# First loads moved to the SyncE queue in f32, with a cast on ScalarE; bv and two combined weights later

## What is computed

```python
q = x @ Wq + bq            # 16 heads of 64
k = x @ Wk + bk            # 2 key heads of 64, 8 query heads share each
v = x @ Wv + bv
scores = q . k over a window of 256 keys, 128 to each side
out    = softmax(scores) @ v
x = layernorm(x + out @ Wo + bo)
# a complex-valued linear layer; W_real and W_imag come from small factors G1, G2
out_real = x_real @ W_real.T - x_imag @ W_imag.T + bias_real
out_imag = x_real @ W_imag.T + x_imag @ W_real.T + bias_imag
x = layernorm(x + concat(out_real, out_imag))
```

## Time and profile before

| | before |
|---|---|
| median of 3 runs | 491.24 us (491.09 to 491.98) |
| profiled execution, its own time | 491.3 us |
| span of its slowest core (core 2) | 489.8 us |
| spans of the 8 cores | 484.1 to 489.8 us |
| TensorE busy | 459.2 us, 94% |
| VectorE busy | 390.8 us, 80% |
| ScalarE busy | 316.8 us, 65% |
| GpSimd busy | 170.0 us, 35% |

### The profile page before, as it was taken

One profiled execution on the slowest core, in us unless ns is written; L12 is line 12 of the kernel. 1 busy time (PEld: TensorE's weight loads), 2 busy tenths in 40 slices (PEclk: granted clock), 3 DMA queues, 4 the chain that ended last, 5 costly groups with the idle time before them and its releaser, 6 DMA issues.

```text
span 489.8 us, 11362 instructions; the slowest of 8 cores (484.1 to 489.8 us)
## 1 busy us (share of the span) xinstructions
PE 459.2 (94%) x3832; PEld 216.9 (44%) x3832; DVE 390.8 (80%) x619; ACT 316.8 (65%) x398; POOL 170.0 (35%) x118
## 2 busy tenths in 40 slices
PE   0698999999999999999999999999999999899994
PEld 0454444444444444444444444444444444344542
DVE  0193678688887988798887988788887888899985
ACT  0136766566776767767676667666766677777653
POOL 8100044343334323443334334432333233333360
PEclk9999999999999999999999999999999999899998
DMA  6999985545664556646664556546642345556333
GB/s 59 160 168 172 217 209 109 108 118 121 150 153 99 140 131 151 144 99 147 151 151 99 134 138 150 136 102 152 151 117 78 111 128 130 153 150 130 87 87 129
DMA packets 82808, 65.15 MB, mean 133 GB/s; under 512 B 67776, under 2 KB 68288, under 8 KB 82752
## 3 DMA queue, kind: packets, MB, share of 16 engines
q1 hardware_dynamic: 75984, 51.17, 40.3%
q0 software_dynamic: 6768, 13.26, 18.4%
HBM read 44.63 MB, written 16.78 MB: 125 GB/s over the span
## 4 chain that ended last, share of the span: by engine, by line
PE 82%; DVE 6%; issue 5%; DMA 3%; ACT 3%; POOL 1%; DVEq 0%; ACTq 0%; POOLq 0%
PE pW L428 22%; PE pW L507 19%; PE pW L493 13%; PE pW L459 9%; PE pS L438 9%; DMA XT<-xt 3%; PE pW L418 3%; PE pW L413 2%; PE pW L476 2%; ACT EX L651 1%; DVE st L805 1%; DVE xb L800 1%; DVE xr L800 1%; PE pS L507 1%; PE pW L402 1%
## 5 line engine op out<-in xcount | busy, mean ns | idle before, releaser
L651 ACT ACTIVATE EX<-pS,shift 128x2048 bf16<-128x2048 f32 x96 | 188.5, 1964 | 58.4 <-PE pS L438 58.4
L376 POOL TENSOR_TENSOR xb<-x,beta_b 128x1024 f32<-128x1024 bf16 x32 | 69.2, 2161 | 159.9 <-DVE x L882 150.9
L428 PE MATMUL pW<-XT,wq_sb 128*128 128x512 bf16 x512 | 120.1, 379 | 0.4 <-DMA XT<-xt 0.2
L507 PE MATMUL pW<-wo_sb,attnT 128*128 128x512 bf16 x496 | 118.2, 384 | 0.0
L384 POOL TENSOR_TENSOR xr<-xr,bo_b 128x1024 f32<-128x1024 f32 x32 | 75.6, 2362 | 121.7 <-DVE EX L777 101.3
L638 ACT ACTIVATE QT<-pW,bq_sb 128x512 bf16<-128x512 f32 x64 | 44.0, 687 | 60.7 <-PE pW L428 59.0
L777 DVE TENSOR_TENSOR EX<-EX,mask_s 128x2048 bf16<-128x2048 bf16 x64 | 80.1, 1252 | 3.3 <-ACT EX L651 3.1
L852 DVE TENSOR_TENSOR xb<-pW,xb 128x1024 f32<-128x1024 f32 x48 | 58.8, 1225 | 17.6 <-PE pW L493 11.2
L507 PEld LDWEIGHTS pW<-wo_sb,attnT 128*128 128x128 bf16 x496 | 45.7, 98 | 60.2 <-issue 14.1
L428 PEld LDWEIGHTS pW<-XT,wq_sb 128*128 128x128 bf16 x512 | 46.0, 98 | 48.4 <-issue 1.8
L459 PEld LDWEIGHTS pW<-VB,EX 128*128 128x128 bf16 x1512 | 50.1, 97 | 27.1 <-issue 26.1
(11 more groups left out here) (77 smaller groups left out, 365.0 us busy)
## 6 DMA issues: line engine op xcount, KB each, us to landing
xr<-x SPq DMA_DIRECT2D x32, 512.0 KB, 3.9
y<-xb SPq DMA_DIRECT2D x31, 512.0 KB, 3.0
XT<-xt POOLq DMA_DIRECT2D x32, 256.0 KB, 5.2
wq_sb<-wq POOLq DMA_DIRECT2D x8, 256.0 KB, 21.8
wo_sb<-wo POOLq DMA_DIRECT2D x4, 512.0 KB, 36.8
bo_b<-bo SPq DMA_DIRECT2D x1, 512.0 KB, 10.5
beta_b<-beta SPq DMA_DIRECT2D x1, 512.0 KB, 5.7
y<-xb SPq DMA_DIRECT2D x2, 256.0 KB, 2.1
```

The source lines that it names most:

```text
L376: gp.tensor_tensor(xb[:, r1 % 4 * D:(r1 % 4 + 1) * D], x1[:, r1 % 2 * D:(r1 % 2 + 1) * D], beta_b, ALU.add).then_inc(gp_b, 1)
L428: i = pe.matmul(p, wq_sb[:, t * 1024 + c * 128:t * 1024 + (c + 1) * 128], rhs_x(g, c), start=c == 0, stop=c == 7)
L507: i = pe.matmul(ps, attnT[:, p % 2 * D + c * 128:p % 2 * D + (c + 1) * 128], wo_sb[:, half * 4096 + c * 512:half * 4096 + (c + 1) * 512], ...
L651: act.activation(EX[:, e0:e0 + 2048], pS, AF.Exp, bias=shift).then_inc(act_e, 1)
```

## The change

wk and x tiles 0 and 1 leave GpSimd's queue. SyncE loads them in f32, as its first three transfers, into `xb`; ScalarE copies each into `wk_sb` or `XT` as bf16 when it has landed, and TensorE's first half waits for the three copies (`act_h`). A tiny instruction ahead of them on ScalarE makes the table load early. dmask goes behind bq and bk; bv goes behind the wait for x tile 3, ahead of mask, and has a semaphore of its own. `wd` moves from the end of step 0 into step 1, `wsn` into step 2. As tiles 0 and 1 no longer count on `d_xt[0]` and `d_xt[1]`, later waits for these expect one round less.

```diff
         def _(sp):
-            sp.dma_start(dmask, dmask_d).then_inc(d_dmask, 16)
+            sp.dma_start(xb[:, 0:D], wk_d).then_inc(d_wk, 16)
+            for t in range(2):
+                sp.dma_start(xb[:, (t + 1) * D:(t + 2) * D],
+                             xt_d[t * 128:(t + 1) * 128, :]).then_inc(d_x0[t], 16)
             sp.dma_start(bq_sb, bq_d).then_inc(d_const, 16)
             sp.dma_start(bk_sb, bk_d).then_inc(d_const, 16)
-            sp.dma_start(bv_b, ap(bv_d, 0, [[0, 128], [1, 128]])).then_inc(d_const, 16)
+            sp.dma_start(dmask, dmask_d).then_inc(d_dmask, 16)
             sp.wait_ge(d_xt[3], 16)
+            sp.dma_start(bv_b, ap(bv_d, 0, [[0, 128], [1, 128]])).then_inc(d_bv, 16)
             sp.dma_start(mask, mask_d).then_inc(d_mask, 16)
...
-            gp.dma_start(wk_sb, wk_d).then_inc(d_wk, 16)
-            load_x(0)
-            load_x(1)
             gp.dma_start(wv_sb, wv_d).then_inc(d_wv, 16)
...
-            pe.wait_ge(d_wk, 16)
...
-                for t in range(2 * h, 2 * h + 2):
-                    pe.wait_ge(d_xt[t], 16)
+                if h == 0:
+                    pe.wait_ge(act_h, 3)
+                else:
+                    pe.wait_ge(d_xt[2], 16)
+                    pe.wait_ge(d_xt[3], 16)
...
-            act.wait_ge(d_const, 3 * 16)
+            act.wait_ge(dve_i, 1)
+            act.activation(nm1[:, 0:1], eps, AF.Copy)
+            act.wait_ge(d_wk, 16)
+            act.activation(wk_sb, xb[:, 0:D], AF.Copy).then_inc(act_h, 1)
+            for t in range(2):
+                act.wait_ge(d_x0[t], 16)
+                act.activation(XT[:, t * D:(t + 1) * D], xb[:, (t + 1) * D:(t + 2) * D], AF.Copy).then_inc(act_h, 1)
+            act.wait_ge(d_const, 2 * 16)
             k_out(0)
...
-            v.wait_ge(d_const, 3 * 16)
+            v.wait_ge(d_bv, 16)
             v_out(0, 4)
...
                     if r < 0:
+                        if s == 1:
+                            v.wait_ge(*emptied(("G", 3)))
+                            v.tensor_tensor(wd, wit, wrt, ALU.subtract).then_inc(dve_g, 1)
+                        if s == 2:
+                            v.tensor_tensor(wsn, witn, wrt, ALU.subtract).then_inc(dve_g, 1)
                         masked(s, 1)
...
                         if s == 0:
                             gate_out(2)
                             gate_out(3)
-                            v.wait_ge(*emptied(("G", 3)))
-                            v.tensor_tensor(wd, wit, wrt, ALU.subtract).then_inc(dve_g, 1)
-                            v.tensor_tensor(wsn, witn, wrt, ALU.subtract).then_inc(dve_g, 1)
```

More of the change, by code:

```diff
@@ L132, in build_nc @@
     d_wk = sem("d_wk")
+    d_bv = sem("d_bv")
+    d_x0 = [sem(f"d_x0_{i}") for i in range(2)]
+    act_h = sem("act_h")
     d_wv = sem("d_wv")
@@ L544, in _ @@
                 if j == 0 and s < Q_END:
-                    new_x = [(d_xt[t % 8], (t // 8 + 1) * 16) for t in range(4 * g + 4, 4 * g + 8)]
+                    new_x = [(d_xt[t % 8], (t // 8 + (1 if t % 8 >= 2 else 0)) * 16) for t in range(4 * g + 4, 4 * g + 8)]
                 else:
@@ L692, in _ @@
                 q_out(n)
-            act.wait_ge(dve_i, 1)
             n_ln = 0
```

## The result

The changed kernel takes 494.56 us (median of 4 runs, 494.19 to 494.82) against 491.24 us before: slower, by a ratio of 1.0067 (95% interval 1.005 to 1.0084). Times and ratios are those of the chip's usual state; single executions in its slower one (here 555.92 us, of the kernel before) are left out. The forecast was 489.5 us with a range of 487.2 to 493.8. Both the sign and the range were missed.

What follows compares the result with a forecast made beforehand. TensorE, busy 94% of the span, bounds the kernel and its head shifts the whole span. Gates at 26.3 + 462.0 - 0.9 = 487.4, plus 0.6 for the worst head: 488.0, plus 1.5 beyond the span: 489.5 us; range 487.2 to 493.8.

Steps and rivals of the forecast that it cites:

- x tile 3: 13.8 forecast: In the head, x tile 3 would land at 13.8 us, with ends of 11.5 and 19.4 us.
- the case of every core: In the head, all cores would be near core 7's undisturbed 15.38 us once bv goes behind x tile 3.
- 1.2 us of free window: From 2.0 to about 3.2 us SyncE's f32 tiles would move at 377 GB/s: 0.86 of a tile, 1.3 us gained.
- part 3: Moving wd and wsn to steps 1 and 2 would end the second av block's wait in step 1: -0.9 us.
- bv's landing: Behind x tile 3, bv would land 7.2 us after its issue, priced by mask's 7.0 us.
- bv lands as late as before: Rival: behind x tile 3 bv takes 12 us; up to 4.8 us more, 492 to 494.3 us; chance 0.12.
- the rival with a gap of 4 us: Rival: TensorE idles some 4 us ahead of the gates; a clock fall costs 1.7 us, giving 488.9; chance 0.14.
- the casts: On ScalarE, 1.24 us each, only the last on the path: x tile 1 cast at 13.2 us.
- core 5's remainder: From the start of the gates block to the end on core 5: 462.0 us, added to the gates' start.
- my own signs of being wrong: Wrong if 72 GB/s stays on some cores, bv takes over 9 us, or gates-to-end is not 459.9 to 462.0 less 0.9.
- The rival that the slow stretch stays: Rival: core 2's 72 GB/s from 7 to 13 us has another cause than bv and stays; 493.8 us; chance 0.14.
- the f32 tiles start at once: Rival: in the head x tile 3 lands at 11.5 us, gates at 24.0, time 487.2 us; chance 0.14.

Runs made afterwards that it cites:

- the two kernels with the one load of constants: Changed kernel with bq, bk and bv in one transfer: 0.9916; kernel before with that transfer, later wd and wsn, gate products first, no f32 loads: 0.9934.
- bv late alone: Kernel before with only bv's load moved behind the wait for x tile 3: 497.1 us, ratio 1.0133.
- part 3 alone: Kernel before with only the two combined weights, wd and wsn, moved to steps 1 and 2: 490.3 us, ratio 0.9986.
- the runs with stored rows: bv stored in HBM as 128 equal rows: in the kernel before, at its old place, 0.9948; in the changed kernel, still behind x tile 3, 1.0039.
- Stored rows for bv alone: Kernel before with bv stored as 128 equal rows and loaded as an ordinary block at the same place: 489.2 us, ratio 0.9948.
- the one load: Kernel before with bq, bk and bv stored side by side as one 128x137 array and loaded in one transfer: 488.4 us, ratio 0.9945.
- the run with stored rows, late: Changed kernel with bv stored as 128 equal rows, still issued behind x tile 3: 492.9 us, ratio 1.0039.
- without the f32 loads: Kernel before with bq, bk and bv in one transfer, wd and wsn later, gate products first; wk and x tiles 0 and 1 on GpSimd's queue: 487.55 us, 0.9934.

## Why the prediction was wrong

The shape was right: the end is the start of the gates plus a constant, VectorE waits for bv, and TensorE waits for VectorE. Three terms were mis-sized, all one way. On core 1 the gates start at 31.25 us instead of the forecast 26.3, 4.95 us later (1.8 + 3.0 + 0.1), and the rest to the end is 461.4 us where the forecast had 462.0 - 0.9 + 0.6 = 461.7; together the 4.7 us between 488.0 and the measured 492.7.

- **x tile 3: 13.8 forecast, 15.6 on core 1, 14.0 to 15.9 on all: 1.8 us.** Two steps failed here. The larger is the one that took core 7 of before as the case of every core once bv was out of the way: on cores 1, 3, 4 and 7 the tile lands behind the stretch of 72 to 80 GB/s from 13 to 15 us, with bv not yet issued (on core 1 bq had landed at 13.1 us, and bk lands at 15.7). The prediction named bk only in a rival. The other booked 1.2 us of free window for the f32 tiles. From 2.0 to 3.2 us they moved at 75 GB/s on core 1, not 377. Other cores show the two apart. Cores 0, 5 and 6, with 232 to 311 GB/s from 2.0 to 3.2 us and no stretch, have x tile 3 at 14.0 to 14.3 us, near the forecast; core 2, with 119 GB/s and no stretch, at 14.8; core 3, with 232 GB/s and the stretch, at 15.6. From 3.2 to 5.0 they ran at 344 GB/s, so the start-up of the other queue did not hold them up; instead that queue delivered its first data later. The two queues (packets, MB written, share of 16 engines) on core 1 in the first 7 us, before and then after:

```profile
q0 software_dynamic: 162, 0.30, 50.6%
q1 hardware_dynamic: 429, 0.14, 10.0%
```

```profile
q1 hardware_dynamic: 271, 1.02, 60.6%
q0 software_dynamic: 11, 0.02, 2.4%
```

Before, 0.30 MB in bf16 are 1.15 tiles; after, 1.02 MB in f32 are 1.95, and 0.02 MB another 0.1. So the lead of 0.9 of a tile that I had booked was there at 7 us. In the two kernels with the one load of constants it was gone by x tile 3: SyncE's next transfer, which waits for this tile, is issued at 15.3 to 16.6 us with the f32 loads and at 15.4 to 16.3 (18.0 on core 4) without. dmask, which was now in between, accounts for an estimated 0.35 us of it (the prediction's sum); the rest was not isolated. With bk and bv loaded by themselves part of the lead did arrive: x tile 3 lands at 14.0 to 15.9 us in the changed kernel, at 14.9 to 17.9 with bv late alone, and the ratios are 1.0067 and 1.0133 (part 3 and dmask's place differ between them too; part 3 alone measured 0.9986). The Trainium skill ("DMA: Bandwidth & Descriptors", "Issuing engines are not separate DMA queues") says that transfers run on the same 16 engines whoever starts them, and that a second issuer saves only the time of issuing. The pair with the one load agrees, 0.9916 and 0.9934 with overlapping intervals; the other pair shows a gain, and why the two differ is open.
- **bv's landing: 7.2 forecast, 10.2 on core 1, 6.9 to 10.2 on all: 3.0 us.** I named bv as the cause of the slow stretch, and then priced bv in its new place by mask, as if the stretch would stay behind. The run with bv late, alone, shows that it travels with bv, and the runs with stored rows show that the repeated row is what does it. The rival "bv lands as late as before" had 0.12; by my own reasoning on the cause it should have been the forecast for the worst core. Its upper end, 494.3 us, even lay outside the range that I gave. The rest of the chain was right within 0.3 us: from issue to gates on cores 0, 2 and 7 it took 12.3 to 12.6 us where I had 12.5.
- **TensorE's clock: nothing forecast, 0.8 to 2.1 us measured.** I priced a fall of the clock only in the rival with a gap of 4 us, and read the 5.31 us of the earlier trace rows as half clock; the mean granted clock over that block is 0.68, so all of it at half clock would cost more than the 1.7 us I took. The idle time ahead of the gates was 2.5 to 4.4 us, because x tile 3 and bv were late, and behind it the clock fell: from 26.6 to 36.0 us the mean granted clock was 0.82 on six cores and 0.64 on two, and 1.00 there before. Core 0, TensorE alone, 27.3 to 30.7 us and after:

```profile
27.30:30.70 3.40, 3.40 (x50) 0.50 1.09 172
30.80:39.00 8.20, 7.47 (x35) 1.00 1.05 168
```

The forty Q matmuls behind the gates took 9.6 to 10.9 us instead of 8.79. On core 1 that took back part 3's 0.9 us, which is why the stretch from the gates to the end looks unchanged. The Trainium skill ("TensorE: Matmul & The Clock Gate", "Part 1: The HAM clock gate (the "warmup" mystery)") says that an idle engine falls back to 1.2 GHz. The trace agrees, 0.50 granted where it was 1.00.

What held: the casts (x tile 1 was cast at 12.8 us on core 1, forecast 13.2), the first halves together on all cores, and part 3 (0.88 us of wait gone, in the change and alone). The remainder from the gates to the end held only by luck: two errors, the clock (+1.0 us on core 1) and the 0.6 us and core 5's remainder that I had added, nearly cancel there. By my own signs of being wrong it had failed: it should have been 459.0 to 461.1 us, and is above 461.1 on seven of eight cores; and bv took over 9 us on four. The rival that the slow stretch stays was given 0.14 and an end at 493.8 us. It came true in part, and in two places: late and short ahead of x tile 3, on four cores, and again behind it, where bv, and with it the gates, had to pass through it. One end of the range was also added up wrongly: 13.8 less 2 us is 11.8, not the 11.5 us of the rival "the f32 tiles start at once", which makes it 487.5 instead of 487.2.

How much of the stretch is bk's and how much bv's was not separated fully. Stored rows for bv alone leave a second K block at 15.0 to 18.5 us, the one load 15.3 to 16.8; so bk has a share, and the 68 to 84 GB/s of three cores in the run with stored rows, late, stand where bk is under way and bv is not; but no kernel here changed bk alone (bq, 32 bytes a partition, went into the one load with it). Why only some cores suffer, and others from run to run, stays open as well. So does the late x tile 3 on core 4 without the f32 loads (18.0 us), where no such stretch is seen.

## What to carry to other kernels

Before moving a small load later, ask what it does to the transfers around it as well as who waits for it. Here one 64 KB load that read the same row 128 times slowed all transfers of some cores, wherever it stood, and the cure was to store the rows (or to put all small constants side by side in one array), not to move it. And when a wait is put ahead of an engine that works in order, price the clock too: gaps of 2.5 to 4.4 us in TensorE cost another 0.8 to 2.1 us behind them. A second queue for the first loads gained nothing measurable here once the small constants came in one load.

## What the runs showed of the hardware

- A repeated 512-byte row, 128 times: while it was under way, core 1 of the changed kernel wrote 87 GB/s and core 2 with bv late, alone, 82 GB/s, for 4 us each. With the same bytes from 128 rows (the run with stored rows, late) no core fell under 134 GB/s in any 2 us from 19 to 25 us.
- One value of 4 bytes to each of 128 partitions (bk, 0.5 KB): 80 and 102 GB/s from 5 to 9 us on core 2 of the run with bv's rows stored, while it was under way; the same core of the one load had 123 and 167 GB/s.
- TensorE's clock after a gap: an idle time of 1.8 and 2.3 us ahead of the gates (cores 7 and 1 of the run with rows stored, late) left it at full, with 8.79 us for the forty Q matmuls; 2.3 us on core 4 of the same run did not (10.42 us, clock 0.59 from 28 to 32 us), nor did 2.5 us and more ahead of the gates in the changed kernel.
- With three f32 tiles ahead on the hardware queue, the casting queue had written 0.02 MB by 7 us on core 1 instead of 0.30.
